# Splitting the r product of a RWKV-style channel mix into three fp32r matmuls, in an adaLN block on one core

## What is computed

```python
x_prev = jnp.concatenate([jnp.zeros((B, 1, C), x.dtype), x[:, :-1, :]], axis=1)
xr = mu_r * x + (1.0 - mu_r) * x_prev
xk = mu_k * x + (1.0 - mu_k) * x_prev
r = jax.nn.sigmoid(jnp.einsum('btc,dc->btd', xr, W_r))
k = jnp.einsum('btc,dc->btd', xk, W_k)
k_act = jnp.square(jax.nn.relu(k))
out = r * jnp.einsum('btc,dc->btd', k_act, W_v)
```

## Time and profile before

| | us |
|---|---|
| median of 3 runs | 747.71 |
| lowest and highest of them | 746.73, 3368.17 |
| the profiled execution | 746.73 |
| its span | 744.9 |
| mean granted clock of TensorE in it | 0.984 |

### The profile page before, as it was taken

One profiled execution on the slowest core, in us unless ns is written; L12 is line 12 of the kernel. 1 busy time (PEld: TensorE's weight loads), 2 busy tenths in 40 slices (PEclk: granted clock), 3 DMA queues, 4 the chain that ended last, 5 costly groups with the idle time before them and its releaser, 6 DMA issues.

```text
span 744.9 us, 11393 instructions
## 1 busy us (share of the span) xinstructions
PE 684.1 (92%) x3554; PEld 545.5 (73%) x3554; DVE 588.1 (79%) x1030; ACT 393.1 (53%) x871; POOL 467.2 (63%) x809
## 2 busy tenths in 40 slices
PE   6958986999999999999999999999999999999797
PEld 2847874888768777788768877697768887687575
DVE  4595879886998699886999679886998869847864
ACT  0323572555745656555645656455655547445653
POOL 4255897568845867558855887557856588407442
PEclk9999998999999999999999999999999999999899
DMA  9213022110311021110221112111220101100002
GB/s 313 83 51 108 1 67 82 36 44 30 93 58 49 29 86 58 60 50 28 63 84 35 42 47 72 56 50 45 75 84 28 50 0 35 39 18 29 29 28 85
DMA packets 40809, 43.21 MB, mean 58 GB/s; under 512 B 2697, under 2 KB 38833, under 8 KB 40785
## 3 DMA queue, kind: packets, MB, share of 16 engines
q1 hardware_dynamic: 38704, 40.24, 16.7%
q10 hardware_dynamic: 2080, 2.68, 1.0%
HBM read 26.06 MB, written 16.85 MB: 58 GB/s over the span
## 4 chain that ended last, share of the span: by engine, by line
POOL 38%; PE 21%; issue 20%; DVE 16%; ACT 2%; DMA 2%; POOLq 1%; DVEq 0%
POOL xb L457 5%; POOL ag L432 3%; POOL y L475 3%; DVE x L861 3%; POOL rs_o L449 3%; DVE t_buf L854 3%; PE work L1267 3%; DVE xk L885 2%; PE work L1250 2%; POOL ag L420 2%; POOL ag_a L432 2%; PE att L1217 2%; POOL wv_aug L464 2%; POOL ag L422 2%; PE gram L1199 2%
## 5 line engine op out<-in xcount | busy, mean ns | idle before, releaser
L1217 PE MATMUL att<-m_sb,z_t 128*128 128x256 f32 x496 | 113.3, 381 | 12.4 <-DVE t_buf L854 10.9
L667 ACT ACTIVATE z<-x,ag 128x256 f32<-128x256 f32 x128 | 66.3, 590 | 92.3 <-POOL ag L442 92.3
L1217 PEld LDWEIGHTS att<-m_sb,z_t 128*128 128x128 f32 x496 | 92.3, 190 | 30.2 <-issue 18.9
L854 DVE SCALAR_TENSOR_TENSOR t_buf<-att,rs_o,g_row 128x256 f32<-128x256 f32 x124 | 51.4, 476 | 75.2 <-POOL rs_o L449 75.2
L1267 PE MATMUL work<-xk,w_k_t 128*128 128x512 f32 x236 | 106.2, 592 | 0.0
L1250 PE MATMUL work<-w_r_t,xr 128*128 128x256 f32 x464 | 104.9, 379 | 0.0
L1250 PEld LDWEIGHTS work<-w_r_t,xr 128*128 128x128 f32 x464 | 86.0, 190 | 10.5
L1101 PE MATMUL work<-wvf_lo,k_hi 128*128 128x256 f32 x248 | 74.6, 301 | 19.7 <-issue 19.7
L457 POOL TENSOR_TENSOR xb<-x_in,rows 128x1024 f32<-128x1024 f32 x32 | 79.2, 2480 | 15.9 <-DMA rows<-row_scratch 8.4
L1199 PE MATMUL gram<-z 128*128 128x256 f32 (+1 forms) x512 | 89.1, 327 | 0.0
L1199 PEld LDWEIGHTS gram<-z 128*128 128x128 f32 x512 | 79.8, 191 | 6.6
(11 more groups left out here) (172 smaller groups left out, 1464.6 us busy)
## 6 DMA issues: line engine op xcount, KB each, us to landing
x_in<-in_L_attn_x_dram SPq DMA_DIRECT2D x32, 512.0 KB, 3.5
out_dram<-y SPq DMA_DIRECT2D x29, 512.0 KB, 3.0
rows<-row_scratch SPq DMA_DIRECT2D x16, 128.0 KB, 3.4
rows<-row_scratch SPq DMA_DIRECT2D x8, 256.0 KB, 3.1
wqkv_sb<-in_L_attn_w_qkv_dram ACTq DMA_DIRECT2D x1, 1536.0 KB, 10.1
x<-in_L_wmod_dram SPq DMA_DIRECT2D x1, 1024.0 KB, 13.1
out_dram<-x_in SPq DMA_DIRECT2D x2, 512.0 KB, 3.0
x<-in_L_wmod_dram SPq DMA_DIRECT2D x1, 512.0 KB, 4.4
```

What stands on the lines that cost most here:

```text
L667: ins = nc.scalar.activation(z2[:, t], x2[:, j, t], ACT.Identity, bias=ag_2[:, s, 1, t:t + 1], scale=ag_2[:, s, 7, t:t + 1])
L854: ins = nc.vector.scalar_tensor_tensor(t_buf[:, t], att_banks(j, alone)[t // 2][:, (t % 2) * D:(t % 2 + 1) * D], rs_o[:, s, t:t + 1], g_ro ...
L1217: ins = mm(att_banks(j, alone)[q][:, (t % 2) * D:(t % 2 + 1) * D], z_t[:, j, k, t * P:(t + 1) * P], m_sb[:, k], start=(k == 0), stop=(k == ...
```

## The change

`ffn_r`, which multiplied xr by `w_r_t` in f32, does it in three fp32r matmuls by `mm3`, as `ffn_out` does. For that xr and W_r are split into a rounded part and a rest. W_r is split once (`w_r_hi` copied by ScalarE in place of `w_r_t`, `w_r_lo` by `split_r` on VectorE). xr is split for each of the 32 chunks: `split_xr` on ScalarE (one copy, 128x1024, fp32r) and `low_xr` on VectorE (one subtraction, 128x1024); `ffn_r` waits for the second. xr has one buffer in place of two, and so have k_hi and k_lo; the last chunk of the last row keeps its k parts in the xr pair. In the last row `ffn_r` no longer waits for the tanh before it, since ScalarE's order with the split covers that.

```diff
+            def split_xr(b, j, alone=False):
+                i = CH * b + j
+                wait_past(act, r_done, 2 * i)
+                act.wait_ge(xr_mixed, i + 1)
+                nc.scalar.activation(xr_hi[:], mixed(j, alone)[0], ACT.Copy).then_inc(xr_hi_ready, 1)
...
                 copy_h2(b, 0)
+                split_xr(b, 0)
                 squares(b, 2)
...
                 copy_z_t(n, 3)
+                split_xr(b, 1)
                 copy_gram(n)
...
                 copy_gq(n)
+                split_xr(b, 2)
                 make_z2(b, 3)
...
                 copy_h2(b, 3)
+                split_xr(b, 3)
...
+            def low_xr(b, j, alone=False):
+                i = CH * b + j
+                dve.wait_ge(xr_hi_ready, i + 1)
+                nc.vector.tensor_tensor(xr_lo[:], mixed(j, alone)[0], xr_hi[:].bitcast(F32), ALU.subtract).then_inc(xr_lo_ready, 1)
...
                 mix(b, 0)
+                low_xr(b, 0)
...
                 mix(b, 1)
+                low_xr(b, 1)
                 gate_o(b, 0)
...
                     stats_a(n + 1, 0)
+                low_xr(b, 2)
                 gate_o(b, 1)
                 softmax_dif(n)
...
                 gate_o(b, 2)
+                low_xr(b, 3)
...
             softmax_norm(0)
+            split_r()
             stats_a(1, 0)
...
             def ffn_r(b, j, alone=False):
-                pe.wait_ge(xr_mixed, i + 1)
+                pe.wait_ge(xr_lo_ready, i + 1)
...
-                        pe.wait_ge(th_ready, 2 * i - 1 + q)
...
-                            ins = mm(r_banks(alone)[q][:, (t % 2) * D:(t % 2 + 1) * D], mixed(j, alone)[0][:, ch, tile], w_r_t[:, ch],
-                                     start=(ch == 0), stop=(ch == KD - 1))
+                            ins = mm3(r_banks(alone)[q][:, (t % 2) * D:(t % 2 + 1) * D],
+                                      (xr_hi[:, ch, tile], xr_lo[:, ch, tile], w_r_hi[:, ch], w_r_lo[:, ch]),
+                                      start=(ch == 0), stop=(ch == KD - 1))
```

More of the change, by code:

```diff
@@ L93, in adaln_block @@
         wfc_c = sb("wfc_c", [P, NP, D])
-        w_r_t = sb("w_r_t", [P, KD, D])
+        w_r_hi = part("w_r_hi", [P, KD, D])
+        w_r_lo = part("w_r_lo", [P, KD, D])
         w_k_t = sb("w_k_t", [P, KD, D])
@@ L146, in adaln_block @@
         h2t = sb("h2t", [P, KD, 1 + L])
-        xr, xk = (sb(n, [P, 2, KD, CT]) for n in ("xr", "xk"))
-        k_hi, k_lo = (part(n, [P, 2, KD, CT]) for n in ("k_hi", "k_lo"))
+        xr = sb("xr", [P, KD, CT])
+        xk = sb("xk", [P, 2, KD, CT])
+        xr_hi, xr_lo, k_hi, k_lo = (part(n, [P, KD, CT]) for n in ("xr_hi", "xr_lo", "k_hi", "k_lo"))
         y = sb("y", [P, 2, NT, D])
@@ L157, in y_buf, with k_split @@
             return x_in[:, j] if alone else y[:, j % 2]
-        def k_split(j):
-            return k_hi[:, j % 2], k_lo[:, j % 2]
+        def k_split(j, alone):
+            return (xr_hi, xr_lo) if alone and j == CH - 1 else (k_hi, k_lo)
         def o_banks(j, alone):
@@ L167, in mixed @@
         def mixed(j, alone):
-            return (z_t[:, 2 * j - CH], z_t[:, 2 * j - CH + 1]) if alone and j >= CH // 2 else (xr[:, j % 2], xk[:, j % 2])
+            return (z_t[:, 2 * j - CH], z_t[:, 2 * j - CH + 1]) if alone and j >= CH // 2 else (xr[:], xk[:, j % 2])
         wmod_sb = x2[:, 0:3].rearrange("p j t d -> p (j t d)").rearrange("p (k n) -> p k n", k=KD)
@@ L727, in last_row @@
                 take_r(b, 1, alone=True)
+                split_xr(b, 2, alone=True)
                 make_z2(b, 3)
@@ L731, in last_row @@
                 take_r(b, 2, alone=True)
+                split_xr(b, 3, alone=True)
                 take_k(b, 2, alone=True)
@@ L946, in prep_qk, with split_r @@
                 ins.then_inc(qk_ready, 1)
+            def split_r():
+                dve.wait_ge(w_copied, 3)
+                nc.vector.tensor_tensor(w_r_lo[:].rearrange("p k d -> p (k d)"), work[0][:],
+                                        w_r_hi[:].rearrange("p k d -> p (k d)").bitcast(F32),
+                                        ALU.subtract).then_inc(w_split, 1)
             def softmax_dif(b):
@@ L1049, in last_row @@
                 mix(b, 2, alone=True)
+                low_xr(b, 2, alone=True)
                 gate_o(b, 0)
@@ L1052, in last_row @@
                 mix(b, 3, alone=True)
+                low_xr(b, 3, alone=True)
                 gate_o(b, 1, alone=True)
@@ L1278, in ffn_out @@
                     pe.wait_ge(ro_ready, 2 * i)
-                hi, lo = k_split(j)
+                hi, lo = k_split(j, alone)
                 for q in range(2):
```

12 lines of the change are left out of this document (8 added, 4 removed).

## The result

The changed kernel takes 775.58 us (median of four runs, 770.9 to 776.2) beside 747.82 us for the kernel before on the same chip: ratio 1.036 (of the means, without one run of the kernel before that took 3368.17 us), 95% interval 1.031 to 1.041. It is slower, 2.6 us above the 773 us forecast.

The account below looks back on a forecast made before the run. It took the batch row's cycle as the bound, some 68 of 86 us on VectorE and GpSimd. Six middle rows at 3.8 us (22.8), row 0 1.8 and last row 1.9 add 26.5 to 746.73: 773 us, range 755 to 785.

Parts of the forecast that it names:

- TensorE's gain: Each ffn_r falls from 3.46 to 2.92 us, 0.55 us a chunk; only ffn_r(b, 2) lies in the cycle's TensorE part.
- place 4: TensorE part of the cycle: ffn_r(b, 2) gives 0.55 us, low_xr(b, 2) meets rstd_2(b, 3); taken as 0.
- Place 1: low_xr(b-1, 3) behind gate_o(b-1, 2): free on VectorE, but holds up GpSimd's rstd_a; 0.95 us a row, between 0 and 1.25.
- Place 2: low_xr(b, 0) behind mix(b, 0): delays GpSimd's rstd_2(b, 1) and xb, so rs_o(b, 2); 1.3 us a row, bounds 0 and 2.0.
- Place 3: low_xr(b, 1) between mix(b, 1) and gate_o(b, 0), where VectorE has no gap: 1.55 us a row, bounds 1.2 and 2.3.
- rival (c): TensorE's clock falls behind the longer wait before ffn_out(b, 1): 2.3 us a row, +14 us, 787 us; chance 0.12.
- The ends: Outside the six middle rows: start 0, row 0 +1.8 us, last row +1.9 us, the two rows each bounded 0 and 4.
- (a): TensorE is the bound, the splits fit into idle time and all 17.5 us come back: 729 us; chance 0.04.
- (b): Places 1 and 2 stay hidden and the 0.55 us counts: 0.65 to 1.5 us a row, 752 to 758 us; chance 0.18.
- (d): ScalarE's queue stands in the splits and low_xr lands behind long GpSimd instructions: 5 us a row, 781 us; chance 0.08.

Follow-up runs that it names:

- e4: Changed kernel with the r product again one f32 matmul for each part, all copies, subtractions and waits kept: 775.96 us, ratio 1.039.
- e1: Changed kernel without the four low_xr subtractions of each row, xr_lo set to zero once: 743.29 us, ratio 0.995.
- e9: Changed kernel with the split kept for chunk 3 alone in the rows before the last, last row as changed: 757.86 us, ratio 1.015.
- e2: Changed kernel with each low_xr replaced by four bn_stats of the same xr, which read one operand: 762.66 us, ratio 1.021.
- e3: Changed kernel without ScalarE's four copies a row, xr_hi zero, subtractions kept: 771.53 us, ratio 1.034.
- e5: Changed kernel with 16 further, useless matmuls on TensorE in the wait before ffn_out(b, 1): 768.56 us, ratio 1.029.
- e14: Changed kernel, but the last row's chunk 2 takes one f32 product without copy and subtraction: 773.08 and 777.66 us in two runs.
- e8: Changed kernel with the split kept for chunk 1 alone in the rows before the last, last row as changed: 769.25 us, ratio 1.030.
- e15: Changed kernel with the split for chunk 2 alone before the last row, none in it, its chunk 1 mixed into free z: 743.20 us, ratio 0.9945.
- e6: Changed kernel with the split kept for chunk 2 alone in the rows before the last, chunk 0 alone in the last: 745.31 us, ratio 0.998.
- e7: Changed kernel with the split kept for chunk 0 alone in the rows before the last, last row as changed: 758.34 us, ratio 1.015.
- e13: Changed kernel with the split kept for chunk 2 alone in the rows before the last, none in the last: 745.08 us, ratio 0.998.

## Why the prediction was right

The mechanism was right: TensorE is fast enough, and what is put on VectorE is paid by the chain. By its steps:

- **TensorE's gain.** 0.55 us a chunk predicted, 0.5 measured, and it counts in one chunk of four, shown by e4 (places 1 to 3 don't move) and e1. I put place 4 at 0 (bounds -0.55 and +1.0), fearing `low_xr(b, 2)`; it is -0.54 at full clock, and +1.0 where the clock falls, the two bounds.
- **Place 1.** 0.95 predicted, 1.11 measured (e9: 1.12), by GpSimd as described (e2 takes it away). VectorE's wait for `rs_o` stayed at 2.48 us, not 2.2: it starts later by as much as it ends later.
- **Place 2.** 1.3 predicted, 1.15 measured. The stretched GpSimd instruction accounts for it: 1.73 us, where it took 0.59 before. The 0.25 more that I gave for xb on the cast isn't there.
- **Place 3.** 1.55 predicted, 1.28 measured. The copy takes 1.05 us, not the 1.16 of the earlier trace rows, and `low_xr` waits 0.1 us for it, not 0.33 (e3: place 3 is 0.11 us shorter without the copy).
- **The clock, rival (c).** The forecast left it out, the rival priced it at 2.3 us in each row. It came in four middle rows of six at 1.45 us. I read 2.3 off row 0, where the clock was down before `ffn_out` began; here it falls inside it. In the profiled execution it adds 5.9 us; with the filler of e5 the six middle rows are 5.6 us shorter (533.6 beside 539.2).
- **The ends.** I had 0 for the start, 1.8 for row 0 and 1.9 for the last row. The start came 1.3 us later, but over the fourteen profiled kernels, most with the same start, the first `m_sb` lies anywhere from 62.9 to 68.2 us, so it can't be told from that spread. Row 0: +1.0. The last row: +4.0, the term sized worst. I had `low_xr(b, 0)`'s wait for the copy, with 2.2 us for what follows (TensorE's `turn_z2(b, 2)` comes 2.5 us later). I hadn't `low_xr(b, 2)` beside `rstd_2(b, 3)`, and not the fall of the clock behind the wait that it lengthens; e14 shows these two to be worth 1.1 and 0.9 us.

Summed for the profiled execution: six rows at 3.02 us are 18.1, the clock 5.9, start 1.3, row 0 1.0, last row 4.0: 30.3, against 30.25 measured (776.98 - 746.73). Predicted were 22.8 + 0 + 1.8 + 1.9 = 26.5. So the forecast's 773 us and the 775.58 us measured lie close partly because errors cancelled: the places were 0.8 us a row too dear, while the clock wasn't counted and the last row only by half.

Rivals (a), (b) and (d) are out: (a) by e4, (b) because places 1 and 2 cost 1.1 us each, (d) by e3 and because only one of the 32 `low_xr` is stretched, to 1.67 us.

What stays open is why a wait of 2.40 us brings the clock down in some rows and not in others: in four of six in the changed kernel's, e2's and e14's profiled executions, in one of six in e3's, in all six of e8's. The last rows of e4 and of the changed kernel differ in the same way behind waits of 1.89 and 1.1 us.

## What to carry to other kernels

Before moving work from a busy TensorE onto VectorE, follow the row's cycle: 92% busy was not the bound, and a saving there counted in one of four places. Count what a VectorE instruction with two SBUF operands does to the small GpSimd instructions beside it; if one lies in the chain, the price is up to the VectorE instruction's length even where VectorE idles. A change that costs when made everywhere may pay where it is free: the split at one chunk of four gives 0.5% (e15; its other products use rounded weights and are a little less exact, and no run keeps the full weights beside the split ones), and the places can be priced one by one, since they add up.

## What was not expected of the hardware

TensorE's granted clock (levels 1.2 and 2.4 GHz) fell to a mean of 0.66 to 0.69 over the 5 us behind waits of 2.40 us, in a stream of work that is otherwise dense; behind waits of 1.7 to 1.96 us in the same place (before, e1, e4, e6, e7, e9, e13, e15) no middle row is longer than the others by such a fall. In the last row of e13 the block behind a wait of 2.14 us took 5.3 us in place of 3.6. One such fall costs 1.4 to 1.7 us, more than any of the four places alone: in e8, where the wait grew by 0.7 us, the fall took more of the row's 2.8 us than the subtraction. A TensorE freed of work can thus run slower: e4 has more TensorE work than the changed kernel, shorter middle rows and the same time, and e5 has 16 idle matmuls more and is 7 us faster.
